# Recurrence gates of a two-layer kernel: twelve compact rows per batch, spread by transfers through memory, and one convolution product moved

## The chip, the cores and the metric

The kernel runs on one core of a Trainium2 chip. The metric is the device time of one execution in microseconds (us); the time before is the median of three executions. The engines are named as in the profile: PE is TensorE, PEld its weight load, DVE VectorE, ACT ScalarE, POOL GpSimd, and SP the engine that here issues most DMA transfers. Float32 is used throughout, and the products that need its accuracy are made as three products of a high and a low part.

## The reference, cut to what matters

Two layers, each a normalisation, an attention-like part, a second normalisation and a feed-forward part, on x of 8 batches x 512 tokens x 256. The change touches only the first part of the first layer, a rotated linear recurrence over 6 heads of 32 pairs:

```python
q, k, v = (causal_depthwise_conv(h @ W, conv) for W, conv in ...)   # [B, T, 6, 64]
theta, psi = q[..., ::2] * inv_freq, k[..., ::2] * inv_freq
alpha = sigmoid(h @ Wa)      # [B, T, 6]: one number per head and token
beta  = sigmoid(h @ Wb)      # [B, T, 6]
def step(state, inp):        # scan over the 512 tokens
    retained  = rotate(state, phi_t) * alpha_t[..., None]
    new_state = retained + beta_t[..., None] * rotate(v_t, psi_t)
    return new_state, rotate(new_state, -theta_t)
o = out * rsqrt(mean(out**2) + eps) * rms_w * silu(h @ Wg)
x = x + o @ Wo
```

alpha and beta have one value per head, but the recurrence runs on 32 pairs of each head, so the kernel needs each of them on 32 partitions. After this part come a router with 16 experts and two shared experts, then the experts' own pass, then a causal attention with 16 heads and a feed-forward part over 688 columns. None of that is changed.

## The kernel before, in words

**Units.** The first layer goes through 4 units (`NU`) of 2 batches each. A unit's 2 x 192 pair rows (6 heads x 32 pairs) are laid on 3 tiles of 128 partitions (`RT = 3`): tile 0 holds heads 0 to 3 of the first batch, tile 2 those of the second, and tile 1 (`SPLIT_ROW`) the last two heads of both, half and half. The free dimension is the 512 tokens.

**Work of a unit y, interleaved with unit x = y - 1.** PE makes for each tile r four convolution products (`conv_products`, q, k and the two halves of v, banks 0 to 3) and the gate products (`gate_products`, banks 4 and 5 in turn, in the order of the list `GATES`). A product of one tile is 6 matmuls of 512 columns; on tile 1 a convolution product is 12. `GATES` has 12 places: places 0 to 5 make the output gates (quantities 4 and 5), places 6 to 11 make alpha and beta (quantities 6 and 7), already repeated for the 32 pairs, because POOL copies each of the 12 weight columns 32 times into `w8raw` at the start. ACT reads each gate bank (`gates`): silu for the output gates; for alpha and beta tanh of half the value and then x0.5 + 0.5, into `al` and `be`. POOL multiplies cos and sin with beta (`beta_taken`), DVE rotates the values with them (`rotate`, six operations on tiles in SBUF) and runs the recurrence as two scans with `al` as the factor (`scan`). ACT squares the result (`squares`), PE sums the squares over each head (`square_sums`, 16 matmuls with 4 columns each), DVE makes the reciprocal root (`rms`), ACT spreads it (`spread_rms`, tile `rexp`), PE transposes it (`rms_turn`), DVE multiplies the gates (`gated`), PE makes the output product (`out_product`) and DVE adds it to x (`residual`). Then come the second norm, the router and the shared experts (`router_turn` to `shared_add`).

**Order.** Each engine's list of work is written out by hand; semaphores tie the engines. On PE the order around the change is: convolution of tile 0, gate places 0 to 3, `square_sums(x, 0)`, places 4 to 7, `square_sums(x, 1)`, places 8 to 11, 12 filler transposes (`clock_turns(MIDDLE_TURNS[0], 7)`, transposes of the identity whose result nobody reads), `square_sums(x, 2)`, the first two convolution products of tile 1, `rms_turn` for three tiles, the other two convolution products, output product, and so on. `al`, `be`, `cs`, `sn`, `ve` and `vo` exist once; unit y writes them when unit x has been scanned (`s_scan`). The start of the kernel is unit 0 alone, with the loads and the clearing of a 10 MB scratch tensor (`tokens_by_expert<-zero`) beside it.

Of the kernel before, what the change touches and what calls it, by code (L numbers as in the profile page):

```python
# [25 lines left out]
P = 128  # L26
# [46 lines left out]
MIDDLE_TURNS = (12, 48, 6)  # L73
# [30 lines left out]
def two_layer_program(nc, x_in, w0, wab, cw, invf, rmsw, wo0, cent, gbias, wexp, iota16, tri, tileno, wpair, fidx, lut, out):  # L104
    ctx = ExitStack()
    with ctx:  # L106
# [8 lines left out]
        x1 = nc.dram_tensor("x1_between_stages", [NB, T, D], F32, kind="Internal").ap()  # L115
        bank = [ctx.enter_context(nc.psum_tensor(f"bank{i}", [P, 512], F32)) for i in range(8)]
# [16 lines left out]
        with ExitStack() as first_layer:  # L133
            def sa(name, shape, dt=F32):
                return first_layer.enter_context(nc.sbuf_tensor(name, shape, dt))

            with ExitStack() as raw:
                w8raw = raw.enter_context(nc.sbuf_tensor("w8raw", [P, KD, 8, ROW], F32))
            ge_even, go_even = (sa(name, [P, RT, T]) for name in ("ge0", "go0"))
            w8 = [sa(f"w8_{part}", [P, KD, 8, ROW], F32R) for part in ("high", "low")]  # L140
# [19 lines left out]
            wabs = sa("wabs", [P, KD, 2, HEADS0])  # L160
# [114 lines left out]
        s_ab = sem("l0_alpha_beta")  # L275
        s_bm = sem("l0_beta_taken")
# [122 lines left out]
        GATES = ((4, 0), (5, 0), (4, 1), (5, 1), (4, 2), (5, 2), (6, 0), (7, 0), (6, 1), (7, 1), (6, 2), (7, 2))  # L399
# [35 lines left out]
        def _(sp):  # L435
# [7 lines left out]
            for dst, src in ((w8raw[:, :, 0:6, :], w0), (wabs[:], wab), (cws[:], cw), (invfs[:], invf)):  # L443
                sp.dma_start(dst, src).then_inc(s_const, 16)
# [17 lines left out]

            for u in range(NU):
                for ab in range(2):
                    sp.wait_ge(s_acc, 2 * u + ab + 1)
                    sp.dma_start(x1[2 * u + ab, :, :].rearrange("(n p) d -> p n d", p=P), xu[u % 3][ab][:]
                                 ).then_inc(s_x1s[u % 3], 16)
                if u + 3 < NU:
                    load_unit(u + 3)
                if u == NU - 2:  # L470
                    sp.wait_ge(s_pv, 12 * NU)
                    sp.wait_ge(s_pg, 12 * NU)
# [62 lines left out]
        def _(pool):  # L535
# [17 lines left out]
            for k in range(KD):  # L553
                for j in range(2):
                    pool.tensor_copy(w8raw[:, k, 6 + j, :].rearrange("p (h c) -> p h c", c=PAIRS),
                                     wabs[:, k, j, :].unsqueeze(2).to_broadcast([P, HEADS0, PAIRS]))
# [3 lines left out]
            def gate_taken(u, r):  # L560
                n = RT * u + r
                pool.wait_ge(s_scan, n + 1)
                pool.wait_ge(s_gr, 12 * u + 2 * r + 2)
# [135 lines left out]
        def _(sc):  # L699
# [54 lines left out]
            def gate_tile(u, quant):  # L754
                return (ge[u % 2], go[u % 2], al, be)[quant - 4]

# [3 lines left out]
            def gates(u, places):  # L760
                for p in places:
                    quant, r = GATES[p]
                    src = bank[4 + p % 2]
                    sc.wait_ge(s_pg, 12 * u + p + 1)
                    if quant >= 6 and u >= 1:
                        sc.wait_ge(s_scan, RT * (u - 1) + r + 1)
                    if r == SPLIT_ROW:
                        first, ab = quant - quant % 2, quant % 2
                        moves = [(gate_tile(u, first + n)[half_of(ab), r, :], src[half_of(n), :]) for n in range(2)]
                    else:  # L770
                        moves = [(gate_tile(u, quant)[:, r, :], src[:])]
                    for dst, part in moves:
                        if quant < 6:
                            ins = sc.activation(dst, part, ACT.Silu)
                        else:
                            ins = sc.activation(dst, part, ACT.Tanh, scale=0.5)
                    ins.then_inc(s_gr, 1)
                for p in places:
                    quant, r = GATES[p]
                    if quant >= 6:  # L780
                        dst = (al, be)[quant - 6][:, r, :]
                        sc.wait_ge(s_gr, 12 * u + p + 1 + (r == SPLIT_ROW and quant % 2 == 0))
                        sc.activation(dst, dst, ACT.Copy, scale=0.5, bias=0.5).then_inc(s_ab, 1)
# [39 lines left out]
            def router_input(u, turns_of=range(4)):  # L823
                for j in turns_of:
# [7 lines left out]
            def shared_silu(u, n):  # L832
# [3 lines left out]
                if n >= 2:  # L836
# [8 lines left out]
            high(w8[0][:, :, 4:8, :].rearrange("p k q n -> p k (q n)"),  # L845
                 w8raw[:, :, 4:8, :].rearrange("p k q n -> p k (q n)"), s_w8h)
# [257 lines left out]
        def _(v):  # L1104
# [319 lines left out]
            for n in range(2):  # L1424
                quants = slice(4 * n, 4 * n + 4)
                v.wait_ge(s_w8h, n + 1)
# [325 lines left out]
        def _(pe):  # L1752
# [44 lines left out]

            def conv_products(u, r, quants):
# [5 lines left out]
            def gate_products(u, places):  # L1804
                for p in places:
                    quant, r = GATES[p]
                    if p >= 2:
                        pe.wait_ge(s_gr, 12 * u + p - 1)
                    elif u == 1:
                        pe.wait_ge(s_gr, 12)  # L1810
                    elif u >= 2:
                        pe.wait_ge(s_acc, 2 * (u - 2) + 1)
                    if r == SPLIT_ROW:
# [16 lines left out]
            def rms_turn(u, r):  # L1830
                pe.wait_ge(s_re, u + 1 + (u == NU - 1 and r >= LAST_PARTS[0][1]))
                if r == 2 and u + 1 < NU:
                    pe.wait_ge(s_gr, 12 * (u + 1) + 11)
# [6 lines left out]
            def out_product(u, ab):  # L1840
                pe.wait_ge(s_y, RT * u + RT)
                if ab == 1 and u + 1 < NU:
                    pe.wait_ge(s_gr, 12 * (u + 1) + 12)
# [33 lines left out]
            def router_turn(u):  # L1877
                pe.wait_ge(s_res, 2 * u + 2)
                unit_turn(u, xm, s_xm, (6, 7, 4, 5), s_t2, (0,))
                clock_turns(MIDDLE_TURNS[2], 5)  # L1880
# [71 lines left out]
            gate_products(0, (6, 7, 8, 9, 10, 11))  # L1952
            first_turn(1)
            pe.wait_ge(s_const2, 16 * CONST2_DMAS)
            for y in range(1, NU):
# [21 lines left out]
                clock_turns(MIDDLE_TURNS[1], 6)  # L1977
# [357 lines left out]
```

## Time and profile before

| | us |
|---|---|
| median of three executions | 2203.79 |
| their lowest and highest | 2198.75, 2204.74 |
| span of the profiled execution, first to last instruction | 2190.4 |
| median less span | 13.4 |
| start and unit 0 alone | 0 to 70 |
| unit pairs y = 1, 2, 3 | 70 to 173.4, to 277.7, to 380.2 |
| last unit's rest, then the experts' pass | 380.2 to about 700 |
| second layer | about 700 to 2190 |

The profiled execution's own time is not recorded apart from its span; the 13.4 us between its span and the median are taken as what lies around a span. PE is busy 97% of the span, DVE 77%, ACT 58% and POOL 26%. The pages give start, duration, engine, line, operation, tiles and, in brackets, the idle time before an instruction with what ended it.

### The profile page before, as it was taken

How to read it: one execution, taken by the hardware profiler on the slowest of the kernel's cores; microseconds unless marked ns; L12 is line 12 of the kernel's file. 1: busy time of each engine (PE TensorE's matmuls, PEld its weight loads, DVE VectorE, ACT ScalarE, POOL GpSimd, SP SyncE). 2: the span in 40 equal slices, each digit the busy share in tenths (PEclk: the TensorE clock that was granted, in tenths of full speed). 3: DMA queues.
4: the chain of work that ended last, by engine and by line, in shares of the span. 5: the costliest groups of instructions: out<-in, count | busy, mean ns of one | idle time of the engine just before them, and what ended most of it. 6: DMA issues, size and time to landing. Idle time of an engine off the chain costs nothing. (4 is left out here: it accounts for less than half of the span.)

```text
span 2190.4 us, 37661 instructions
## 1 busy us (share of the span) xinstructions
PE 2123.2 (97%) x13038; PEld 1854.3 (85%) x13038; DVE 1694.3 (77%) x4387; ACT 1273.8 (58%) x3487; POOL 559.2 (26%) x604
## 2 busy tenths in 40 slices
PE   6899999979999999999999999999999999999997
PEld 5677777758788999899989989998998999899887
DVE  7998886887767887777876877787687778767775
ACT  5644443226637676666665666666566666656662
POOL 0214333430015323122222312222232222222220
PEclk9999999999999999999999999999999999999999
DMA  9001010436522112112111211211121121111100
GB/s 300 1 1 58 20 46 26 170 121 205 172 68 64 59 51 76 39 52 70 54 40 55 82 39 54 69 54 39 57 80 39 54 68 54 39 58 50 39 20 20
DMA packets 88556, 145.81 MB, mean 67 GB/s; under 512 B 8369, under 2 KB 55857, under 8 KB 88369
## 3 DMA queue, kind: packets, MB, share of 16 engines
q1 hardware_dynamic: 67904, 112.73, 16.1%
q0 software_dynamic: 6144, 16.79, 2.2%
q10 hardware_dynamic: 14320, 13.90, 1.9%
q8 instruction: 106, 1.74, 0.3%
q14 instruction: 82, 0.66, 0.1%
HBM read 105.63 MB, written 37.75 MB: 65 GB/s over the span
## 5 line engine op out<-in xcount | busy, mean ns | idle before, releaser
L1018 ACT ACTIVATE pr<-bank,negmax 128x128 f32<-128x128 f32 (+3 forms) x512 | 263.5, 527 | 196.6 <-DVE negmax L1599 196.6
L653 POOL TENSOR_TENSOR wo_low<-wraw_o,wo_high 128x256 fp32r<-128x256 f32 x128 | 94.5, 738 | 1105.0 <-ACT wo_high L705 1105.0
L1136 DVE TENSOR_TENSOR p_low<-bank,p_high 128x512 fp32r<-128x512 f32 (+2 forms) x384 | 190.2, 551 | 100.6 <-ACT p_high L705 100.0
L705 ACT ACTIVATE p_high<-bank 128x512 fp32r<-128x512 f32 (+2 forms) x384 | 177.4, 497 | 149.9 <-PE bank L2121 149.9
L1599 DVE CUSTOM_DVE_ANT_0 bank<-bank,causal 128x128 f32<-128x128 f32 (+3 forms) x512 | 234.7, 520 | 1.1 <-PE bank L1762 1.1
L1626 DVE SCALAR_TENSOR_TENSOR xs<-bank,rinv,xs 128x256 f32<-128x256 f32 x512 | 211.7, 474 | 1.2 <-PE bank L1762 1.2
L1760 PE MATMUL bank<-h_high,wqk_high 128*128 128x512 f32 x512 | 202.6, 396 | 0.0
L1761 PE MATMUL bank<-h_low,wqk_high 128*128 128x512 f32 x512 | 202.5, 396 | 0.0
L1762 PE MATMUL bank<-h_high,wqk_low 128*128 128x512 f32 x512 | 202.3, 395 | 0.0
L1136 DVE TENSOR_TENSOR z_low<-bank,z_high 128x512 fp32r<-128x512 f32 x128 | 88.4, 691 | 130.8 <-ACT z_high L705 130.3
L643 POOL TENSOR_TENSOR wqk_low<-wraw,wqk_high 128x512 fp32r<-128x512 f32 x128 | 165.6, 1294 | 77.3 <-ACT wqk_high L705 77.3
L2121 PEld LDWEIGHTS bank<-ident,pr 128*128 128x128 f32 x1280 | 147.6, 140 | 18.4 <-ACT pr L1018 1.3
L2121 PE MATMUL bank<-ident,pr 128*128 128x128 f32 x1280 | 160.4, 272 | 1.1 <-ACT pr L1018 1.1
L705 ACT ACTIVATE z_high<-bank 128x512 fp32r<-128x512 f32 x128 | 76.6, 599 | 138.1 <-PE bank L2132 138.1
L1760 PE MATMUL bank<-wv_high,h_high 128*128 128x256 f32 x512 | 154.8, 302 | 0.0
L1760 PE MATMUL bank<-wo_high,z_high 128*128 128x256 f32 x512 | 148.0, 289 | 2.4 <-issue 2.3
L1762 PE MATMUL bank<-wv_high,h_low 128*128 128x256 f32 x512 | 144.5, 282 | 0.0
L1762 PE MATMUL bank<-wo_high,z_low 128*128 128x256 f32 x512 | 144.1, 282 | 0.0
L1761 PE MATMUL bank<-wv_low,h_high 128*128 128x256 f32 x512 | 144.0, 281 | 0.0
L1761 PE MATMUL bank<-wo_low,z_high 128*128 128x256 f32 x512 | 143.8, 281 | 0.0
L1760 PE MATMUL bank<-k_high,q_high 128*128 128x384 f32 (+2 forms) x384 | 140.8, 367 | 0.0
L1760 PE MATMUL bank<-p_high,v_high 128*128 128x512 f32 (+2 forms) x384 | 131.2, 342 | 2.4 <-DVE p_low L1136 2.3
(338 smaller groups left out, 6327.3 us busy)
## 6 DMA issues: line engine op xcount, KB each, us to landing
wraw<-in_wpair SPq DMA_DIRECT2D x64, 512.0 KB, 4.0
wraw<-in_wpair SPq DMA_DIRECT2D x64, 256.0 KB, 4.4
wraw_o<-in_wpair SPq DMA_DIRECT2D x64, 256.0 KB, 2.5
tokens_by_expert<-zero SPq DMA_DIRECT2D x10, 1024.0 KB, 11.2
xt<-tokens_by_expert SPq DMA_DIRECT2D x40, 256.0 KB, 3.3
expert_results<-ey ACTq DMA_DIRECT2D x40, 256.0 KB, 3.7
wres<-in_wexp SPq DMA_DIRECT2D x1, 6144.0 KB, 20.7
xs<-x_between_stages SPq DMA_DIRECT2D x8, 512.0 KB, 4.5
```

The source lines that it names most:

```text
L643: pool.tensor_tensor(low, wraw[r][:, 2 * e * D:2 * (e + 1) * D], high.bitcast(F32), ALU.subtract).then_inc(s_wq, 1)
L653: pool.tensor_tensor(wo2[e][1][:], wraw_o[r][:, e, :], wo2[e][0][:].bitcast(F32), ALU.subtract).then_inc(s_wo, 1)
L705: sc.activation(dst, src, ACT.Copy, scale=scale).then_inc(done, 1)
L1018: ins = sc.activation(pr[:, i, 0:(i + 1) * P], score(i), ACT.Exp, scale=-1.0, bias=negmax[:, i:i + 1], accum_out=rsum[:, i:i + 1])
L1136: v.tensor_tensor(at(parts[1]), src, high_, ALU.subtract).then_inc(done, 1)
L1599: ins = v.tensor_tensor_reduce(score(i), score(i), causal[:, (NT - 1 - i) * P:NT * P], -1.0, -NEG, ALU.add, ALU.min, negmax[:, i:i + 1])
L1626: ins = v.scalar_tensor_tensor(xb[:, i, :], bank[6 + n][:, (i % 2) * D:(i % 2 + 1) * D], rinv[:, i:i + 1], xb[:, i, :], ALU.mult, ALU.add)
L1760: mm(dst, w[0], x[0], start=start, stop=False)
L1761: mm(dst, w[0], x[1], start=False, stop=False)
L1762: return mm(dst, w[1], x[0], start=False, stop=stop)
L2121: ins = pe.transpose(bank[2 + n][:, at:at + P], pr[:, i, j * P:(j + 1) * P], ident[:])
```

## The change

alpha and beta are no longer made on all pair rows. Their 12 weight columns (6 for alpha, 6 for beta) are kept as they are, padded to 64 columns (`wab2`), and one product of 6 matmuls per batch gives 12 rows of 512 tokens. ACT applies the same tanh and x0.5 + 0.5 to these 12 rows (`alpha_beta`, into `ab_rows`, which lies in the first 12 partitions of `hm`). SP stores the rows of a unit in a small tensor in memory (`ab_heads`), waits until they are there, waits until `al` and `be` are free, and loads them back with eight transfers (`spread_alpha_beta`), each of which reads every row 32 times, so that they fill `al` and `be`. `beta_taken` waits for all eight. `GATES` has 8 places. POOL's four copies of weight columns are gone, the conversions of the weights are smaller, and the 12 filler transposes are gone. On PE the products of q and k of tile 1 (`conv_products(y, 1, (0, 1))`) are issued ahead of `square_sums(x, 2)` instead of behind it, and ACT reads them behind `squares(x, 2)`, where it did before. A tensor `room` keeps the addresses behind the smaller weights where they were.

```diff
-MIDDLE_TURNS = (12, 48, 6)
+MIDDLE_TURNS = (48, 6)
+        ab_heads = nc.dram_tensor("alpha_beta_by_head", [2, 2, HEADS0, T], F32, kind="Internal").ap()
...
-                w8raw = raw.enter_context(nc.sbuf_tensor("w8raw", [P, KD, 8, ROW], F32))
+                w8raw = raw.enter_context(nc.sbuf_tensor("w8raw", [P, KD, 6, ROW], F32))
+                wabs = raw.enter_context(nc.sbuf_tensor("wabs", [P, KD, P // 2], F32))
+            wab2 = [sa(f"wab_{part}", [P, KD, P // 2], F32R) for part in ("high", "low")]
+            sa("room", [P, 10 * P])
+            ab_rows = hm[0:2 * HEADS0, 0]
...
-        GATES = ((4, 0), (5, 0), (4, 1), (5, 1), (4, 2), (5, 2), (6, 0), (7, 0), (6, 1), (7, 1), (6, 2), (7, 2))
+        GATES = ((4, 0), (5, 0), (4, 1), (5, 1), (4, 2), (5, 2), (6, 0), (6, 1))
+        NG0 = len(GATES)
+        AB_PIECES = ((0, 0, P, 0, 0, 4), (1, 0, P // 2, 0, 4, HEADS0), (1, P // 2, P, 1, 4, HEADS0), (2, 0, P, 1, 0, 4))
+        AB_DMAS = 2 * len(AB_PIECES)
...
+            def spread_alpha_beta(u):
+                sp.wait_ge(s_ab, 2 * u + 2)
+                sp.wait_ge(s_abr, 16 * AB_DMAS * u)
+                sp.dma_start(ab_heads.rearrange("b q h t -> (q h) b t"), ab_rows).then_inc(s_abw, 16)
+                sp.wait_ge(s_abw, 16 * (u + 1))
+                if u >= 1:
+                    sp.wait_ge(s_scan, RT * u)
+                    sp.wait_ge(s_bm, RT * u)
+                for q, dst in enumerate((al, be)):
+                    for r, p0, p1, ab, h0, h1 in AB_PIECES:
+                        sp.dma_start(dst[p0:p1, r, :],
+                                     ab_heads[ab, q, h0:h1, :].unsqueeze(1).to_broadcast([h1 - h0, PAIRS, T])
+                                     ).then_inc(s_abr, 16)
+
+            spread_alpha_beta(0)
             for u in range(NU):
+                if u + 1 < NU:
+                    spread_alpha_beta(u + 1)
...
             def beta_taken(u, r):
                 pool.wait_ge(s_trig, RT * u + r + 1)
-                pool.wait_ge(s_ab, 6 * u + 2 * r + 2)
+                pool.wait_ge(s_abr, 16 * AB_DMAS * (u + 1))
...
+            def alpha_beta(u):
+                if u >= 1:
+                    sc.wait_ge(s_abw, 16 * u)
+                    sc.wait_ge(s_su, 4 * max(u - 1, 0))
+                for ab in range(2):
+                    p = 6 + ab
+                    sc.wait_ge(s_pg, NG0 * u + p + 1)
+                    sc.activation(ab_rows[:, ab, :], bank[4 + p % 2][0:2 * HEADS0, :], ACT.Tanh, scale=0.5).then_inc(s_gr, 1)
+                for ab in range(2):
+                    sc.wait_ge(s_gr, NG0 * u + 7 + ab)
+                    sc.activation(ab_rows[:, ab, :], ab_rows[:, ab, :], ACT.Copy, scale=0.5, bias=0.5).then_inc(s_ab, 1)
...
             def router_input(u, turns_of=range(4)):
+                sc.wait_ge(s_abw, 16 * min(u + 2, NU))
...
-            gates(0, (6, 7))
+            alpha_beta(0)
             whole_turns(0, 2)
-            gates(0, (8, 9))
             input_high(1)
             sin_cos(0, 2)
-            gates(0, (10, 11))
...
                 squares(x, 1)
-                gates(y, (6, 7))
-                gates(y, (8, 9))
-                gates(y, (10,))
+                alpha_beta(y)
                 squares(x, 2)
-                gates(y, (11,))
                 tap_angle(y, 1)
                 spread_rms(x)
...
+            def alpha_beta_product(dst, ab):
+                for k in range(KD):
+                    ins = mm3(dst[0:P // 2, :], parts(wab2, lambda t: t[:, k, :]), parts(hT2, lambda t: t[:, ab, k, :]),
+                              k == 0, k == KD - 1)
+                return ins
...
-            gate_products(0, (6, 7, 8, 9, 10, 11))
+            gate_products(0, (6, 7))
             first_turn(1)
...
                 gate_products(y, (4, 5, 6, 7))
                 square_sums(x, 1)
-                gate_products(y, (8, 9, 10, 11))
-                clock_turns(MIDDLE_TURNS[0], 7)
+                conv_products(y, 1, (0, 1))
                 square_sums(x, 2)
-                conv_products(y, 1, (0, 1))
                 for r in range(RT):
                     rms_turn(x, r)
```

## Rows read from the trace of the kernel before

**Rows 1.** Stretches: busy time of each engine, granted PE clock, DMA share, GB/s.

```profile
core 0: us, PE busy (x) PEld busy (x) DVE busy (x) ACT busy (x) POOL busy (x), PEclk, DMA share, GB/s
0.00:70.00 70.00, 48.31 (x205) 37.10 (x206) 57.45 (x122) 42.73 (x73) 9.68 (x22) 1.00 0.71 234
70.00:173.40 103.40, 97.49 (x498) 75.05 (x498) 91.00 (x190) 50.12 (x87) 25.06 (x41) 0.98 0.01 3
```

**Rows 2.** DVE timeline, pairs y = 1, 2, 3: around rms and residual.

```profile
105.38 0.21 DVE L1125 SCALAR_TENSOR_TENSOR ry<-rt,ry 128x48 f32<-128x48 f32 x1
107.95 2.32 DVE L1180 SCALAR_TENSOR_TENSOR ang<-bank,cws,ang 128x511 f32<-128x511 f32 x3 [2.37 <-ACT ang L723]
...
134.07 1.29 DVE L1274 TENSOR_TENSOR xs<-bank,xs 128x512 f32<-128x512 f32 x2 [1.90 <-PE bank L1855]
...
208.27 0.21 DVE L1125 SCALAR_TENSOR_TENSOR ry<-rt,ry 128x48 f32<-128x48 f32 x1
...
311.47 0.21 DVE L1258 TENSOR_SCALAR va<-bank 128x48 f32<-128x48 f32 x1 [1.39 <-PE bank L1827]
```

**Rows 3.** PE and ACT timelines: the roots' transposes of the three pairs, and the spread.

```profile
109.80 1.47 PE L1836 MATMUL bank<-ident,rexp 128*128 128x128 f32 x12
...
211.28 1.47 PE L1836 MATMUL bank<-ident,rexp 128*128 128x128 f32 x12
...
316.89 1.47 PE L1836 MATMUL bank<-ident,rexp 128*128 128x128 f32 x12
...
107.81 1.48 ACT L797 ACTIVATE rexp<-ry 128x1536 f32<-128x1536 f32 x1
```

**Rows 4.** Stretches as in rows 1: same products warm and cold, two more falls.

```profile
102.80:109.80 7.00, 7.00 (x26) 4.85 (x27) 4.04 (x14) 2.57 (x4) 0.00 (x0) 0.79 0.00 0
205.70:211.30 5.60, 5.60 (x27) 3.91 (x27) 4.20 (x15) 2.57 (x4) 4.09 (x5) 1.00 0.23 94
...
249.40:256.00 6.60, 6.60 (x14) 3.70 (x15) 4.59 (x22) 3.69 (x5) 2.48 (x2) 0.50 0.00 0
```

**Rows 5.** PE timeline, pair 1: last sums of squares, whose start waited for ACT.

```profile
100.78 0.38 PE L1826 MATMUL bank<-headsum,sq 128*128 128x4 f32 x2 [0.78 <-ACT sq L791]
```

**Rows 6.** ACT and POOL timelines, unit 0: last step of beta, then POOL's use.

```profile
57.98 0.64 ACT L783 ACTIVATE be<-be 128x512 f32<-128x512 f32 x1
...
58.77 1.29 POOL L572 TENSOR_TENSOR cs<-cs,be 128x512 f32<-128x512 f32 x1 [46.57 <-ACT be L783]
60.02 1.26 POOL L572 TENSOR_TENSOR sn<-sn,be 128x512 f32<-128x512 f32 x1
...
71.48 1.40 POOL L572 TENSOR_TENSOR cs<-cs,be 128x512 f32<-128x512 f32 x1 [4.23 <-ACT be L783]
72.85 1.73 POOL L572 TENSOR_TENSOR sn<-sn,be 128x512 f32<-128x512 f32 x1
```

**Rows 7.** DVE timeline, 69 to 88 us: first rotation beside POOL, second without.

```profile
69.85 0.67 DVE L1228 TENSOR_TENSOR tt<-ve,cs 128x512 f32<-128x512 f32 x1
...
71.65 1.78 DVE L1231 TENSOR_TENSOR tt<-ve,sn 128x512 f32<-128x512 f32 x1
73.47 1.66 DVE L1232 TENSOR_TENSOR tt<-tt 128x512 f32<-128x512 f32 x1
75.05 0.68 DVE L1233 TENSOR_TENSOR tt<-tt 128x512 f32<-128x512 f32 x1
...
83.48 0.69 DVE L1228 TENSOR_TENSOR tt<-ve,cs 128x512 f32<-128x512 f32 x1
...
87.34 1.22 DVE L1240 TENSOR_TENSOR_SCAN oe<-al,tt 128x512 f32<-128x512 f32 x1
```

**Rows 8.** DMA issues to 440 us (KB each, median us to landing); one issue on SP.

```profile
x_between_stages<-xs SPq DMA_DIRECT2D x3, 512.0 KB, 3.0
...
tokens_by_expert<-xm,slots POOLq DMA_INDIRECT x48, 2.4
...
8.84 0.43 SPq L449 DMA_DIRECT2D luts<-in_lut  x1
```

**Rows 9.** Stretches as in rows 1: rate of plain transfers, and of indirect ones.

```profile
30.00:50.00 20.00, 20.00 (x88) 14.88 (x87) 18.85 (x45) 12.98 (x25) 0.00 (x0) 1.00 1.04 341
...
207.00:208.00 1.00, 1.00 (x6) 0.60 (x5) 0.85 (x5) 0.00 (x0) 0.74 (x1) 1.00 0.32 131
```

More of the change, by code:

```diff
@@ L137, in two_layer_program @@
             with ExitStack() as raw:
-                w8raw = raw.enter_context(nc.sbuf_tensor("w8raw", [P, KD, 8, ROW], F32))
+                w8raw = raw.enter_context(nc.sbuf_tensor("w8raw", [P, KD, 6, ROW], F32))
+                wabs = raw.enter_context(nc.sbuf_tensor("wabs", [P, KD, P // 2], F32))
             ge_even, go_even = (sa(name, [P, RT, T]) for name in ("ge0", "go0"))
-            w8 = [sa(f"w8_{part}", [P, KD, 8, ROW], F32R) for part in ("high", "low")]
+            w8 = [sa(f"w8_{part}", [P, KD, 6, ROW], F32R) for part in ("high", "low")]
+            wab2 = [sa(f"wab_{part}", [P, KD, P // 2], F32R) for part in ("high", "low")]
+            sa("room", [P, 10 * P])
             ge_odd, go_odd = (sa(name, [P, RT, T]) for name in ("ge1", "go1"))
@@ L159, in two_layer_program @@
             wo_rest = sa("wo_rest", [P, 2, D])
-            wabs = sa("wabs", [P, KD, 2, HEADS0])
             cws = sa("cws", [P, 2, 4, TAPS])
@@ L275, in two_layer_program @@
         s_ab = sem("l0_alpha_beta")
+        s_abw = sem("l0_alpha_beta_stored")
+        s_abr = sem("l0_alpha_beta_spread")
         s_bm = sem("l0_beta_taken")
@@ L442, in _ @@
             load_unit(0)
-            for dst, src in ((w8raw[:, :, 0:6, :], w0), (wabs[:], wab), (cws[:], cw), (invfs[:], invf)):
+            for dst, src in ((w8raw[:], w0), (wabs[:], wab), (cws[:], cw), (invfs[:], invf)):
                 sp.dma_start(dst, src).then_inc(s_const, 16)
@@ L471, in _ @@
                     sp.wait_ge(s_pv, 12 * NU)
-                    sp.wait_ge(s_pg, 12 * NU)
+                    sp.wait_ge(s_pg, NG0 * NU)
                     for c in range(EARLY_CHUNKS):
@@ L552, in _ @@
             pool.wait_ge(s_const, 16 * CONST_DMAS)
[L553 to L556, printed above, removed]
             pool.tensor_scalar(cws[:, :, 0], cws[:, :, 0], invfs[:, 0:1], -1.0, ALU.mult, ALU.mult)
@@ L562, in gate_taken @@
                 pool.wait_ge(s_scan, n + 1)
-                pool.wait_ge(s_gr, 12 * u + 2 * r + 2)
+                pool.wait_ge(s_gr, NG0 * u + 2 * r + 2)
                 for gate, scanned in ((ge, oe), (go, oo)):
@@ L752, in sin_cos @@
                 sc.activation(cs[:, r, :], turns[n % 2][:], ACT.Sin, scale=-1.0, bias=half_pi[:]).then_inc(s_trig, 1)
-            def gate_tile(u, quant):
-                return (ge[u % 2], go[u % 2], al, be)[quant - 4]
             def half_of(n):
@@ L763, in gates @@
                     src = bank[4 + p % 2]
-                    sc.wait_ge(s_pg, 12 * u + p + 1)
-                    if quant >= 6 and u >= 1:
-                        sc.wait_ge(s_scan, RT * (u - 1) + r + 1)
+                    sc.wait_ge(s_pg, NG0 * u + p + 1)
                     if r == SPLIT_ROW:
-                        first, ab = quant - quant % 2, quant % 2
-                        moves = [(gate_tile(u, first + n)[half_of(ab), r, :], src[half_of(n), :]) for n in range(2)]
+                        ab = quant % 2
+                        moves = [(gate[u % 2][half_of(ab), r, :], src[half_of(n), :]) for n, gate in enumerate((ge, go))]
                     else:
-                        moves = [(gate_tile(u, quant)[:, r, :], src[:])]
+                        moves = [((ge, go)[quant - 4][u % 2][:, r, :], src[:])]
                     for dst, part in moves:
[L773 to L776, printed above, removed]
+                        ins = sc.activation(dst, part, ACT.Silu)
                     ins.then_inc(s_gr, 1)
[L778 to L783, printed above, removed]
+            def alpha_beta(u):
[4 more added lines that the diff above has]
+                    p = 6 + ab
+                    sc.wait_ge(s_pg, NG0 * u + p + 1)
+                    sc.activation(ab_rows[:, ab, :], bank[4 + p % 2][0:2 * HEADS0, :], ACT.Tanh, scale=0.5).then_inc(s_gr, 1)
+                for ab in range(2):
+                    sc.wait_ge(s_gr, NG0 * u + 7 + ab)
+                    sc.activation(ab_rows[:, ab, :], ab_rows[:, ab, :], ACT.Copy, scale=0.5, bias=0.5).then_inc(s_ab, 1)
             def squares(u, r):
@@ L844, in _ @@
             sc.wait_ge(s_setup, 2)
-            high(w8[0][:, :, 4:8, :].rearrange("p k q n -> p k (q n)"),
-                 w8raw[:, :, 4:8, :].rearrange("p k q n -> p k (q n)"), s_w8h)
+            high(wab2[0][:], wabs[:], s_w8h)
+            high(w8[0][:, :, 4:6, :].rearrange("p k q n -> p k (q n)"),
+                 w8raw[:, :, 4:6, :].rearrange("p k q n -> p k (q n)"), s_w8h)
             input_high(0)
@@ L1424, in _ @@
             for n in range(2):
-                quants = slice(4 * n, 4 * n + 4)
-                v.wait_ge(s_w8h, n + 1)
+                quants = slice(4 * n, min(4 * n + 4, 6))
+                v.wait_ge(s_w8h, 2 * n + 1)
+                if n == 1:
+                    v.tensor_tensor(wab2[1][:], wabs[:], wab2[0][:].bitcast(F32), ALU.subtract)
                 v.tensor_tensor(w8[1][:, :, quants, :], w8raw[:, :, quants, :], w8[0][:, :, quants, :].bitcast(F32),
@@ L1807, in gate_products @@
                     if p >= 2:
-                        pe.wait_ge(s_gr, 12 * u + p - 1)
+                        pe.wait_ge(s_gr, NG0 * u + p - 1)
                     elif u == 1:
-                        pe.wait_ge(s_gr, 12)
+                        pe.wait_ge(s_gr, NG0)
                     elif u >= 2:
                         pe.wait_ge(s_acc, 2 * (u - 2) + 1)
-                    if r == SPLIT_ROW:
+                    if quant == 6:
+                        alpha_beta_product(bank[4 + p % 2], r).then_inc(s_pg, 1)
+                    elif r == SPLIT_ROW:
                         rests_product(bank[4 + p % 2], quant - quant % 2, quant % 2).then_inc(s_pg, 1)
@@ L1832, in rms_turn @@
                 if r == 2 and u + 1 < NU:
-                    pe.wait_ge(s_gr, 12 * (u + 1) + 11)
+                    pe.wait_ge(s_gr, NG0 * (u + 1) + NG0 - 1)
                 for i in range(NT):
@@ L1842, in out_product @@
                 if ab == 1 and u + 1 < NU:
-                    pe.wait_ge(s_gr, 12 * (u + 1) + 12)
+                    pe.wait_ge(s_gr, NG0 * (u + 1) + NG0)
                 half = slice(ab * P // 2, (ab + 1) * P // 2)
@@ L1879, in router_turn @@
                 unit_turn(u, xm, s_xm, (6, 7, 4, 5), s_t2, (0,))
-                clock_turns(MIDDLE_TURNS[2], 5)
+                clock_turns(MIDDLE_TURNS[1], 5)
                 unit_turn(u, xm, s_xm, (6, 7, 4, 5), s_t2, (1,))
@@ L1976, in _ @@
                 pe.wait_ge(s_res, 2 * x + 1)
-                clock_turns(MIDDLE_TURNS[1], 6)
+                clock_turns(MIDDLE_TURNS[0], 6)
                 router_turn(x)
@@ L2279 @@
     w0 = kt(w0.reshape(D, -1)).reshape(P, KD, 6, ROW)
-    wab = kt(np.concatenate([a["L0_attn_Wa"], np.roll(a["L0_attn_Wb"], HEADS0 - P // PAIRS, -1)], 1)).reshape(P, KD, 2, HEADS0)
+    wab = kt(np.concatenate([a["L0_attn_Wa"], a["L0_attn_Wb"], np.zeros((D, P // 2 - 2 * HEADS0), np.float32)], 1))
     cq, ck, cv = (a["L0_attn_conv_" + c].T for c in "qkv")
```

## The prediction, made blind

> **What bounds the kernel now.** I read the page's busy shares first, then the stretches, then the timelines of DVE, PE, ACT and POOL side by side. Only the first layer, the first 480 us or so, can change. In the start and in the pairs y = 1 to 3 the engine that sets the pace is mostly DVE: 91.00 of 103.4 us busy in pair 1 [rows 1], and without a gap from 70 to 102.7 us. Then there is a place where the pace passes to PE. In pair 1 the chain of the reciprocal root ends at 105.59 (105.38 + 0.21), DVE waits 2.37 us for the q angle of tile 1, and later 1.90 us for the output product before the second residual [rows 2]. Between, PE runs without a gap from the roots' transposes at 109.80 [rows 3] to that product. So what counts in a pair is how early PE can start `rms_turn`; everything behind moves with it, because PE's 48 filler transposes that come later only fill a wait for DVE's second norm. ACT and POOL have slack, so the ten ACT instructions per unit that disappear are worth nothing by themselves: what hides them is DVE's unbroken work.
>
> **PE's work.** Places 8 to 11 go: 4 x 6 = 24 matmuls, and 12 filler transposes. The 24 matmuls of the moved products q and k take their place; a run of 24 takes 5.6 us warm with what is around it [rows 4]. The alpha-beta products at places 6 and 7 stay at 6 matmuls each, as long as before, since the columns streamed are still 512. Up to `square_sums(x, 2)` PE has thus the same work, less the fillers, and all of this lies under DVE's rotations. The gain is behind the sums: PE no longer has 5.6 us (7.0 in pair 1) between sums and transposes.
>
> **The pairs' gain.** `rms_turn` now waits for the root and its spread alone: the end of DVE's chain, 0.1 us to ACT, 1.48 us for `rexp` [rows 3], 0.1 us to PE, so 1.7 us behind the chain's end.
> Pair 1: DVE's wait of 0.30 us before the chain goes too (the sums start earlier, ACT being free for the squares at once, where PE waited 0.78 us [rows 5]). Chain end 105.59 - 0.3 = 105.3; transposes at 107.0 instead of 109.80 [rows 3]: 2.8 us.
> Pair 2: chain end 208.48 [rows 2]; transposes at 210.2 instead of 211.28: 1.1 us.
> Pair 3: the chain starts without its wait of 1.39 us [rows 2]. In the same distances it ends at 312.7, transposes at 314.4 instead of 316.89: 2.5 us.
> Sum 6.4 us, if PE's clock holds. DVE is not in the way: it does the q angle (2.3 us) and the gates while PE does its products, and the 1.90 us of waiting at the residual say that PE has to be earlier first.
>
> **The clock.** The same moved products take 7.0 us at a mean granted clock of 0.79 in pair 1 and 5.6 us at 1.00 in pair 2 [rows 4]: a fall to the lower level (1.2 GHz) costs 1.4 us there. It fell behind a wait of 0.78 us followed by the 4-column matmuls [rows 5], and behind the same pattern in pair 2 it did not. Now PE has, behind those sums, nothing at all from about 101.5 to 107.0, five to six us without fillers. I take it that the clock is down at `rms_turn` in each pair. The price of one fall lies between 1.4 us (dense products) and 3.3 us, half of the 6.6 us that it stayed at 0.50 at 249.4 [rows 4]; I take 1.8 us, nearer the first, because dense products follow. Three falls: 5.4 us. Falls elsewhere I keep as they are. The pairs thus give 6.4 - 5.4 = 1.0 us. Bounds: 6.4 us gained, 3.5 us lost.
>
> **The start, where cover is missing.** In unit 0 there is no earlier unit under which the way through memory could hide. beta of tile 0 was ready at 58.62 (57.98 + 0.64) and used by POOL at 58.77 [rows 6]; the rotation began at 69.85 [rows 7]. Now ACT has the 12 rows of both batches at about the same 58.6: the same two products before it and the same four instructions, whose length goes by the 512 columns and not by the partitions. Then, on SP, whose queue is idle there (the clearing has been issued by 46 us and landed by 53):
> - the store, 48 KB: between 2.4 and 3.0 us to landing [rows 8]; I take 3.0, at 61.7 with SP's wake-up.
> - eight loads, 0.43 us each to issue [rows 8], the last at 65.1; 1.57 MB at 341 GB/s need 4.6 us, at 131 GB/s 12.0 us [rows 9]. With some 2.5 us from first issue to first data and landing, 68.3 by the first; by the second 61.7 + 12.0 + about 1 = 74.7. No row has a load that reads a row 32 times. I take the first rate, since these are plain transfers with 2 KB pieces issued by SP, and the slow one is POOL's indirect scatter, which its issue paces.
> - POOL's two multiplications, 2.5 us [rows 6]: cos and sin ready at 70.9. The rotation starts at 70.9 instead of 69.85: 1.0 us lost. DVE itself would be ready about 68, because the last angle reduction no longer runs beside POOL.
> - what is late next: tiles 1 and 2 of beta come now straight behind, so four POOL instructions fall on the first rotation's six DVE operations instead of two. Rows: the six operations took 5.9 us (69.85 to 75.76) with two POOL instructions beside them and 3.9 us (83.48 to 87.34) with none, so 1.0 us for each [rows 7, 6]. Four cost 4.1 instead of 2.0: 2.1 us lost.
>
> The start loses 3.1 us. The smaller weight conversions (768 + 128 columns instead of 1536 on ACT and DVE) and POOL's four copies give nothing I would count: DVE's first angle waits for PE's first product.
>
> The Trainium skill (SBUF — State Buffer, section "SBUF: two separate sides") says that the pair of ports that DVE and GpSimd share is an exclusive lock, held for the whole instruction, also against DVE operations with two SBUF inputs. By that rule each POOL instruction would hold DVE for its full 1.27 us, four for 5.1 us, and the sum would be 0.9 us higher. The rows show alternation as the rule has it, and 1.0 us for each, which I use. The same skill (DMA: Bandwidth & Descriptors, section "Anatomy of one DMA — SWDGE (gpsimd) path") puts the fixed cost of a transfer at about 2.0 us, most of it completion. By that figure the small store would land 1.0 us earlier, and the sum would be as much lower.
>
> **Later units' transfers.** SP sends the store of unit y at about 93 us in pair 1, waits for the third scan at 98.3 and the eight loads land by 105; `beta_taken` needs the first cosine at about 109. Even at the slow rate (111) only POOL waits, and the rotation comes 65 us later. Behind SP's new waits stand the x1 stores and the load of unit 3, which wait anyway for `shared_add` at 171 us. So 0. The wait in `router_input` for the store is long past. Without this cover the price would be that of the start.
>
> **Sum.** +3.1 - 1.0 = +2.1 us on the span of 2190.4, so 2192.5; with the 13.4 us around it 2205.9, against the median of 2203.8.
>
> **The rivals.**
> *A. The spread is slow (slower).* Loads that read one row 32 times go at 131 GB/s or below: landing at 74.7, 6.4 us later than above, all on DVE's path: +8.5, 2212.3. It decides from a landing at 72.8 on. For it: no row shows such a load. Against it: 341 GB/s for plain transfers, idle queues. Chance 0.18.
> *B. The clock holds at `rms_turn`.* In pair 2 it held over a short gap. Then 6.4 gained, 3.1 lost: -3.3, 2200.5; if the loads also land by the time DVE is ready, the start loses 1 us and it is -5.4. Against it: the gap is now many times as long. Chance 0.15.
> *C. The falls at the router move.* The clock fell at 249.4 and not at the same place of pair 1, so everything that shifts by some us may add or remove one; DVE lost about 2.8 us by it. Two fewer: -5.6 + 2.1 = -3.5, 2200.3; with B in any pair beyond that. One or two more: +4.9 to +7.7, 2208.7 to 2211.5. Chance 0.10 for fewer, 0.07 for more.
> *D. The likeliest*, the sum above, 2200 to 2212 by its own bounds: 0.50.
>
> **Chances and range.** 0.3%, 6.6 us, is about what a measurement here can tell from no change: the three runs lie 6 us apart. Faster by more needs parts of B and C together: 0.12. Slower by more: most of A, some of C's second half and the dear end of D, 0.25. Between: 0.63. The range that holds 8 in 10 reaches from B and C together with one fall fewer (2200.5 - 2.8, 2197.7) to A with falls at 2.4 us instead of 1.8 (2212.3 + 1.8, 2214.1): 2197 to 2214.
>
> **What the changed profile would show.** The store of `ab_heads` issued near 58.7, the last load landed near 68, POOL's six multiplications of unit 0 in one row from there, and the first rotation from about 71 to 79 with several operations near 1.7 us. In each pair: no wait before the q angle, `rms_turn` 1.7 us behind the root's chain, about 5 us of idle PE ahead of it, and a granted clock of 0.5 for some us behind it; the second residual still waiting for PE. Behind 480 us nothing. The prediction is wrong if the loads land after 72.8, if the clock stays at 1.00 at the transposes, or if the number of falls at the router differs.

## The result, and the profile after

The changed kernel takes 2226.7 us (2225.8 to 2230.6, 4 runs) against 2201.9 us for the kernel before in the same series (4 runs): ratio 1.0112, 95% interval [1.0099, 1.0125], which on a time of 2198 us is 24.6 us slower. The forecast was 2205.9, and its range ended at 2214. Every execution after takes 1.7 us more than its span (2225.81 and 2224.1 in the profiled one). So the trace of before, span 2190.4, was of an execution near 2192, 4 to 10 us under the medians that this kernel shows in the four series (2195.8 to 2201.9); the 13.4 us of the forecast were mostly that. Differences between traces thus overstate a loss by some 6 us. Below, losses of whole kernels go by the ratios; stretches inside a kernel are read from single traces.

The trace shows two places. The first is unit 0. SP's timeline of after has store and loads (the last column but one is how many transfers a row holds):

```profile
57.62 0.37 SPq L475 DMA_DIRECT2D alpha_beta_by_head<-hm  x1
59.46 2.47 SPq L482 DMA_DIRECT2D al<-alpha_beta_by_head  x4
61.98 9.45 SPq L482 DMA_DIRECT2D be<-alpha_beta_by_head  x4
```

Stretches of after, while the loads run (the last three numbers are the granted PE clock, the DMA share and GB/s):

```profile
63.00:68.00 5.00, 5.00 (x20) 4.59 (x21) 4.35 (x7) 3.11 (x6) 0.00 (x0) 0.52 0.26 99
76.00:78.00 2.00, 0.00 (x0) 0.00 (x0) 0.00 (x0) 0.00 (x0) 0.00 (x0) 1.00 0.13 51
80.00:82.00 2.00, 0.00 (x0) 0.00 (x0) 0.00 (x0) 0.00 (x0) 0.00 (x0) 0.50 0.12 46
```

A share of 0.26 is 4 of the 16 DMA engines, 0.13 is 2. The pieces of 4 heads (1.05 MB) and of 2 heads (0.52 MB) take 1.05/0.100 + 0.52/0.051, about 10.5 + 10.3 = 20.8 us, from 61 to 82. This sums the pieces as if they ran one after another. The stretches don't follow the order of the pieces (0.26 up to 69 us, 0.13 to 72, about 0.26 to 75, 0.13 to 82), so some overlap. If the same two engines take part in every piece, each carries 8 x 65.5 KB, and at 25 GB/s that is 21.0 us, as long. Which engine carried what isn't shown. POOL's timeline of after has the first use of beta, DVE's the first rotation, the answer to [rows 6, 7]:

```profile
82.56 1.26 POOL L594 TENSOR_TENSOR cs<-cs,be 128x512 f32<-128x512 f32 x1 [72.17 <-DMA be<-alpha_beta_by_head]
```

```profile
85.08 1.73 DVE L1245 TENSOR_TENSOR tt<-ve,cs 128x512 f32<-128x512 f32 x1 [17.07 <-POOL sn L594]
86.74 1.74 DVE L1246 TENSOR_TENSOR tt<-vo,sn 128x512 f32<-128x512 f32 x1
...
91.85 0.69 DVE L1249 TENSOR_TENSOR tt<-tt 128x512 f32<-128x512 f32 x1
```

DVE is ready at 68.0 and waits 17.07 us; before, it had rotated since 69.85. Four of six operations then take 1.74 us beside POOL.

The second place is pairs 2 and 3. POOL's timeline of after in pair 2, then ACT's, PE's and DVE's:

```profile
245.78 1.28 POOL L594 TENSOR_TENSOR cs<-cs,be 128x512 f32<-128x512 f32 x1 [15.38 <-DMA be<-alpha_beta_by_head]
247.03 1.26 POOL L594 TENSOR_TENSOR sn<-sn,be 128x512 f32<-128x512 f32 x1
248.46 1.01 POOL L605 DMA_INDIRECT tokens_by_expert<-xm,slots  x1 [0.16 <-issue]
...
262.40 0.96 POOL L605 DMA_INDIRECT tokens_by_expert<-xm,slots  x1 [0.31 <-issue]
```

```profile
264.80 2.08 ACT L734 ACTIVATE xm<-xs,nbu,ryu 128x256 f32<-128x256 f32 x4 [6.93 <-DMA tokens_by_expert<-xm,slots]
```

```profile
267.02 1.94 PE L1798 MATMUL bank<-ident,xm 128*128 128x128 f32 x8 [4.64 <-ACT xm L734]
```

```profile
275.92 0.29 DVE L1309 TENSOR_SCALAR bia<-bank 128x128 f32<-128x128 f32 x1 [6.39 <-PE bank L1914]
```

Read downwards this is one chain. Ten of the 16 scatters of unit y-2 stand behind the late beta in POOL's program; they read `xm`, so `router_norm` of unit y-1 can't write it; PE waits for the transposes' input, DVE for the logits. Pair 1 has no scatters and is hardly longer.

In each pair the roots' transposes, the answer to [rows 3], take 2.8 us instead of 1.47, with the granted clock at 0.50 (PE's timeline of after; stretches of after behind the first):

```profile
125.05 2.83 PE L1863 MATMUL bank<-ident,rexp 128*128 128x128 f32 x12 [4.28 <-ACT rexp L817]
...
228.48 2.82 PE L1863 MATMUL bank<-ident,rexp 128*128 128x128 f32 x12 [5.26 <-ACT rexp L817]
...
338.17 2.82 PE L1863 MATMUL bank<-ident,rexp 128*128 128x128 f32 x12 [5.13 <-ACT rexp L817]
```

```profile
123.00:129.00 6.00, 3.95 (x16) 3.66 (x17) 5.37 (x10) 3.14 (x4) 0.00 (x0) 0.50 0.22 79
129.00:133.00 4.00, 4.00 (x18) 2.81 (x17) 3.86 (x7) 0.69 (x1) 0.00 (x0) 0.97 0.21 80
```

### The profile page after: what moved, and what is told of

Read it like the earlier page. It is cut to its first block and busy times, and to the rows that moved or that the text cites. A ratio compares the mean times of both kernels' runs of the same rounds, so it can differ in the third digit from the quotient of the medians.

```text
span 2224.1 us, 37388 instructions
## 1 busy us (share of the span) xinstructions
PE 2115.3 (95%) x12906; PEld 1845.9 (83%) x12906; DVE 1695.3 (76%) x4388; ACT 1249.6 (56%) x3448; POOL 558.5 (25%) x600
## 6 DMA issues: line engine op xcount, KB each, us to landing
wres<-in_wexp SPq DMA_DIRECT2D x1, 6144.0 KB, 20.8
```

## The experiments

All are compared with the kernel before on the same chip. "First scan" is the start of the odd scan of tile 0 in unit 0 on DVE's timeline, the pairs are the distances to the same scan of units 1, 2 and 3, and the last stretch is from there to the first `xt` transposes on PE. These are of one trace each. "Loss" is (ratio - 1) x 2198 us, so a width of 0.0018 in an interval is 4 us.

| kernel | first scan | pairs 1, 2, 3 | last stretch | ratio [95%] | loss |
|---|---|---|---|---|---|
| before | 76.9 | 103.1, 104.3, 102.5 | 90.4 | | |
| the change | 94.3 | 104.0, 109.9, 105.8 | 94.9 | 1.0112 [1.0099, 1.0125] | 24.6 |
| e1 wide stores | 84.9 | 103.3, 103.0, 102.8 | 90.4 | 1.0012 [1.0002, 1.0021] | 2.6 |
| e2 move alone | 77.0 | 109.0, 107.3, 102.8 | 93.9 | 1.0053 [1.0036, 1.0069] | 11.6 |
| e3 e1 + fillers | 84.5 | 102.9, 100.4, 98.5 | 92.3 | 1.0011 [1.0001, 1.0021] | 2.4 |
| e4 scatters first | 94.5 | 103.6, 102.9, 102.7 | 90.4 | 1.0060 [1.0039, 1.0081] | 13.2 |
| e5 e1 without the move | 84.6 | 106.5, 103.5, 102.5 | 92.0 | 1.0033 [1.0019, 1.0047] | 7.3 |
| e6 a load per head | 84.1 | 103.7, 102.9, 102.7 | 90.4 | 1.0006 [0.9995, 1.0018] | 1.3 |
| e7 early alpha-beta | 74.7 | 105.6, 105.8, 102.7 | 90.3 | 0.9981 [0.9970, 0.9992] | -4.2 |
| e8 e7 + fillers | 74.6 | 101.6, 100.3, 98.5 | 92.4 | 0.9961 [0.9946, 0.9977] | -8.6 |
| e9 two copies | 86.4 | 102.7, 102.8, 100.3 | 92.1 | one run, 2201.7 against 2198.1 | |
| e10 slow loads in unit 0 alone | 94.3 | 103.1, 102.9, 99.5 | 90.5 | 1.0046 [1.0028, 1.0064] | 10.1 |
| e11 slow loads in units 1 to 3 alone | 83.5 | 103.1, 109.7, 106.3 | 90.4 | 1.0059 [1.0041, 1.0077] | 13.0 |

**e1, wide stores.** Two stores write each of the 12 rows 8 times; the loads' outer dimension becomes 32 or 16.

```
+for ab in range(2):
+    sp.dma_start(ab_heads[ab]..., ab_rows[:, ab, :].unsqueeze(1).to_broadcast([2 * HEADS0, 8, T]))
-ab_heads[ab, q, h0:h1, :].unsqueeze(1).to_broadcast([h1 - h0, PAIRS, T])
+ab_heads[ab, q, h0:h1, :, :].rearrange("h c t -> (h c) t").unsqueeze(1).to_broadcast([(h1 - h0) * 8, PAIRS // 8, T])
```

> The changed kernel, but the store writes each of the 12 rows eight times into memory and each load reads rows 16 or 32 deep in its outer dimension (repeated 4 times instead of 32). Same bytes loaded, 1.57 MB per unit, eight loads as before. Theory 1 (a load runs on as many DMA engines as its outer dimension, 4 heads or 2, allows; the profile shows 0.26 and 0.13 of the engines busy at 100 and 50 GB/s): the busy share goes above 0.8, the last load of unit 0 lands between 66 and 71 us instead of 82.5, the first rotation starts near 70 to 72 instead of 85, the scatters of units 2 and 3 are no longer late, and the time is 2200 to 2207. Theory 2 (reading the same memory row again and again is what is slow): the rate stays near 100 GB/s at best, the landing stays behind 78 us and the time behind 2218.

Stretches of e1, stores and then loads, and PE's timeline:

```profile
59.00:64.00 5.00, 1.08 (x5) 1.11 (x6) 4.79 (x7) 0.28 (x1) 0.00 (x0) 0.50 0.67 77
...
66.00:72.00 6.00, 6.00 (x25) 4.85 (x24) 1.61 (x3) 3.18 (x6) 0.00 (x0) 0.85 0.77 259
```

```profile
114.82 2.82 PE L1865 MATMUL bank<-ident,rexp 128*128 128x128 f32 x12 [5.30 <-ACT rexp L819]
```

The share rises from 0.26 and 0.13 to 0.77 in the mean while the loads run, beta is taken at 73.04 instead of 82.56, and 22.0 of the 24.6 us are gone. The share of above 0.8 and the landing by 71 were missed, though not by much. The wider stores take until 64 us, so the loads are issued from 64.64 on instead of 59.46.

**e2, the move alone**, in the kernel before: `conv_products(y, 1, (0, 1))` ahead of `square_sums(x, 2)`, without the 12 fillers.

> The kernel before with one part of the change alone: the products of q and k of tile 1 ahead of the last sums of squares, and the 12 filler transposes gone; alpha and beta as before. If the step of the prediction holds, the roots' transposes start 1.1 to 2.8 us earlier in each pair and a fall of the clock behind the idle stretch takes about 1.8 us of it back each time: 2198 to 2203 against some 2202 for the kernel before. If the clock's fall costs more than the earlier start gives (up to 3.3 us each), 2203 to 2207. If the clock holds: 2195 to 2197.

DVE's waits in e2 (us in total, times, the longest):

```profile
DVE va L1258 <- PE bank L1827: 13.9, 3, 6.2
```

All three expected times were too low (2207.5 beside 2195.8). With the 24 matmuls of places 8 to 11 still there, the moved ones make the sums late and DVE waits for them, which the expectation had left out. The move needs the compact rows.

**e3, fillers.** e1 with `clock_turns(38, 7)` between `square_sums(x, 2)` and `rms_turn`.

> As the kernel with wide loads, and 38 filler transposes (4.3 us) between the last sums of squares and the roots' transposes of each pair, where PE is idle. If the clock's fall at that place costs what I think, the granted clock is 1.00 at the roots' transposes and the time 4 to 6 us below that of the kernel with wide loads. If the fall costs nothing (DVE sets the pace there), equal within 2 us.

In these two traces the pairs shrink by 7.2 us in all, 2.4 for each fall avoided. The time hardly moves: by the medians e3 is 0.7 us faster than e1 (2197.28 and 2197.93), where 4 to 6 were expected. The last stretch takes 1.9 us more, and what comes after the layer 2 us more (2195.8 - 478.6 = 1717.2 against 2199.4 - 484.3 = 1715.1). The trace of e1 is also of an execution 3.2 us above its median, so the 2.4 us may be too high.

**e4, the scatters first.** The change, but POOL issues all 16 scatters ahead of the multiplications by beta.

> The changed kernel with narrow loads, but in the pairs 2 and 3 POOL issues all 16 scatters of the earlier unit ahead of the three multiplications with beta instead of between them. Theory A (the late beta holds POOL, behind it stand the scatters, and ACT may not overwrite xm before they are done): ACT's wait for the scatters (6.9 us in pair 2) goes, and the time falls by 5 to 10 us to 2217 to 2222; the start stays as late as it is. Theory B (the late scatters cost nothing, the loss behind the start is the clock's): within 2 us of 2226.7.

PE's waits in e4, and the change's wait for the same input beside it:

```profile
PE bank L1798 <- ACT xm L734: 0.5, 3, 0.2
```

```profile
PE bank L1798 <- ACT xm L734: 8.0, 4, 4.6
```

The chain through POOL's queue is shown: betas come as late as in the change, the first scan too, and pairs 2 and 3 are 103 us long. It is worth 11.4 us (24.6 - 13.2), more than the 5 to 10 expected.

**e5, no move.** e1 with the moved products back behind the sums, without fillers.

> Compact rows with every row stored eight times (so that the loads' outer dimension is 16 or 32), and the products q and k of tile 1 back behind the last squares' sums; the 12 fillers stay out. Theory (the cost of the compact rows is the wait of unit 0 for beta, and the move by itself is worth about 1 us): start as in the run with wide stores, first scan about 8 us later than before, and the pairs about as long as before's (sum 309 to 311 us), rms_turn with a clock of 1.00 because products lie ahead of it; the whole 0 to 3 us slower than the wide run with the move. Rival (the move costs more than it gives, by the clock at rms_turn): the pairs shorter than the wide run's by 3 us or more, and the whole faster than it by as much.

e5 is 4.7 us slower than e1, more than the 0 to 3 expected: with compact rows the move gives some 5 us, though it lets the clock fall. In e5 the roots' transposes take 0.27 us each, in e1 0.42.

**e6, a load per head.** The change's single store, then 24 loads.

```
-sp.dma_start(dst[p0:p1, r, :], ab_heads[ab, q, h0:h1, :].unsqueeze(1).to_broadcast([h1 - h0, PAIRS, T]))
+for h in range(h0, h1):
+    p = p0 + PAIRS * (h - h0)
+    sp.dma_start(dst[p:p + PAIRS, r, :], ab_heads[ab, q, h:h + 1, :].to_broadcast([PAIRS, T]))
```

> The change with its single store of 48 KB, but 24 loads of one head each (outer dimension 32, 64 KB) instead of eight loads of 2 or 4 heads. Theory (a transfer's rate goes by how its outer dimension divides over the 16 engines: 4 heads 100 GB/s, 2 heads 50 GB/s in the change): issue sets the pace, 24 x 0.43 = 10.3 us from about 60, so the last lands near 73, the later units' beta comes in time, and the kernel is within 4 us of the wide run and some 25 us faster than the change. Rival (a load that reads a row 32 times is slow as such, whatever its shape): 1.57 MB at 50 to 100 GB/s again, landing at 80 or later, and a time near the change's.

Stretch of e6 while its loads run:

```profile
62.00:72.00 10.00, 8.90 (x38) 7.86 (x39) 5.39 (x9) 4.62 (x8) 0.00 (x0) 0.73 0.53 138
```

The same bytes, the same rows read 32 times, from the same 48 KB, now at 138 GB/s: 64 KB every 0.46 us, the pace of issue. Reading a row 32 times isn't what was slow. POOL takes beta at 72.28. Nearly the whole loss is gone.

**e9, two copies.** e1 with 2 copies of each row, so that the outer dimension is 8 or 4.

> As the run with wide stores, but every row stored twice, so that the loads' outer dimension is 8 for the pieces of 4 heads and 4 for those of 2. Theory (the outer dimension sets how many of the 16 DMA engines carry a load): 4-head pieces at a DMA share near 0.5 and 200 GB/s, 2-head pieces at 0.25 and 100 GB/s, twice the change's rates; 1.05 MB and 0.52 MB take 5.2 + 5.2 = 10.4 us instead of 20.8, beta of tile 0 is taken by POOL near 73, first scan 84 to 86. Rival (reading a row many times from memory is slow by the repeated reads, not by the shape): the shares stay at 0.26 and 0.13, the landing near 80.

```profile
66.00:70.00 4.00, 4.00 (x16) 3.18 (x15) 1.72 (x3) 3.39 (x6) 0.00 (x0) 0.70 0.51 178
...
72.00:74.00 2.00, 2.00 (x10) 1.65 (x9) 0.00 (x0) 0.00 (x0) 0.00 (x0) 1.00 0.25 90
```

Twice the change's shares. Outer dimension 2, 4, 8 gives shares of 0.13, 0.26, 0.51. The theory expected these, with the landing a little earlier (POOL takes beta at 74.66).

**e10 and e11, the two halves.** The change's eight loads in unit 0 alone, or in units 1 to 3 alone; elsewhere a load per head.

> The change with its eight loads in unit 0 and 24 loads of one head each in the units 1 to 3. Theory (the change loses in two places: some 15 us at the start, and 10 to 13 us where late betas hold POOL and with it the scatters of the unit before): the first scan late as in the change, 94 to 95, the pairs 103 to 104 us each, 2208 to 2213, as the run with the scatters first. Rival (the scatters' order mattered, not the late betas): pairs as long as the change's and a time near 2225.

> The other half: 24 loads of one head each in unit 0, the change's eight loads in the units 1 to 3. Theory: first scan at 84, pairs 2 and 3 longer than 103 us by what the change showed there (109.9 and 105.8), last stretch 94 to 95, 2208 to 2213: the two losses add up to the change's. Rival (the late betas only hurt because unit 0 had already been late): pairs near 103 and a time near that of 24 loads everywhere, 2198.

POOL's waits from 90 us on, e10 and then e11:

```profile
POOL cs L606 <- DMA be<-alpha_beta_by_head: 17.8, 3, 11.6
```

```profile
POOL cs L606 <- DMA be<-alpha_beta_by_head: 51.3, 3, 20.6
```

Against e6 the slow loads cost 8.8 us in unit 0 and 11.7 us in the later units; with e6's own 1.3 this makes 21.8 of the 24.6 us. The intervals of e10 and e11 reach 4 us to either side, so the remaining 2.8 us are not clear of noise. e11 shows that late betas in later units hurt by themselves, without a late start. Its last stretch was expected at 94 to 95 us, as in the change, and took 90.4.

**e7, alpha-beta early.** e1 with the alpha-beta products as places 0 and 1 of a unit, and unit 0's store and loads issued ahead of the clearing.

```
-GATES = ((4, 0), (5, 0), (4, 1), (5, 1), (4, 2), (5, 2), (6, 0), (6, 1))
+GATES = ((6, 0), (6, 1), (4, 0), (5, 0), (4, 1), (5, 1), (4, 2), (5, 2))
+spread_alpha_beta(0)
 for n in range(NTILE // 8):
     sp.dma_start(xsort[...], zero[...])
```

> Wide stores, and the alpha-beta product as the first instead of the last of the eight gate products of a unit, with unit 0's store and loads issued ahead of the clearing of the sorted tokens. Theory (what the compact rows cost at the start is that nothing lies over their way through memory): beta lands before DVE is ready to rotate; the first rotation starts at 70 or earlier and the first scan is back near before's 76.9; pairs as in the wide run (309.0 in all); some 7 us faster than the wide run, so 2188 to 2193, 3 to 7 us faster than the kernel before. Rival: the clearing, now some 10 us later, or the gates of the second and third tile, now later, hold DVE or POOL instead, and nothing is won over the wide run.

POOL's timeline of e7:

```profile
44.78 1.28 POOL L596 TENSOR_TENSOR cs<-cs,be 128x512 f32<-128x512 f32 x1 [34.35 <-DMA be<-alpha_beta_by_head]
```

The way through memory is hidden, and the first scan starts 2.2 us earlier than before. Against e1 it wins 10.2 us there and 6.8 by the ratios; its pairs are 5 us longer than e1's, where they were expected to be equal, and no run tells why.

**e8, the same with fillers**: `clock_turns(38, 7)` as in e3.

> As the run before, with 38 filler transposes between the last squares' sums and rms_turn. Theory (the fall of the clock at rms_turn costs 1.8 us in each pair or more): the pairs take 302 to 305 us instead of 309, and 2182 to 2190 in all. Rival (what is won in the pairs is given back where the last unit waits for something else, as in the wide run with fillers): the pairs shorter, the end of the layer not, and a time equal to the run without fillers.

Stretches around `rms_turn` in the three pairs, e7 and then e8:

```profile
100.00:115.00 15.00, 10.43 (x40) 8.19 (x41) 13.68 (x28) 4.44 (x7) 2.52 (x2) 0.66 0.20 65
205.00:220.00 15.00, 9.67 (x37) 7.50 (x38) 13.59 (x28) 3.82 (x5) 12.15 (x12) 0.66 0.43 150
310.00:325.00 15.00, 9.65 (x40) 7.58 (x40) 13.77 (x29) 3.83 (x5) 12.21 (x13) 0.66 0.47 169
```

```profile
100.00:115.00 15.00, 15.00 (x84) 12.94 (x82) 13.91 (x29) 5.67 (x8) 2.55 (x2) 0.89 0.18 60
205.00:220.00 15.00, 14.18 (x72) 11.17 (x71) 14.51 (x21) 5.41 (x8) 10.01 (x10) 1.00 0.24 94
310.00:325.00 15.00, 15.00 (x67) 11.77 (x66) 14.34 (x24) 4.91 (x8) 8.10 (x8) 1.00 0.11 44
```

The mean clock is 0.66 without fillers and 0.89 to 1.00 with them. The pairs shrink by 13.6 us in these two traces, but the medians differ by 5.4 (2191.96 and 2186.55); the trace of e7 is of an execution 4.1 us above its median. e7 and e8 both beat the kernel before. e8 is the faster, 2186.6 us, and even the upper end of its interval is 0.23% under the kernel before. Why the same fillers gave 5.4 us here and 0.7 in e3 isn't shown.

## Why the prediction was wrong, step by step

The forecast said +2.1 us, the ratio says +24.6. The error of 22.5 us has three parts that the runs measure: 14.3 at the start, 11.7 in the later units, and 4.2 the other way in the pairs. That makes 21.8; the rest is within the noise.

**The rate of the loads: the step that failed.** "I take the first rate, since these are plain transfers with 2 KB pieces issued by SP": 341 GB/s, landing at 68.3. Measured: 100 and 51 GB/s, POOL released at 82.56. The row it rested on [rows 9] is of the clearing, stores from 128 partitions; these are loads with an outer dimension of 4 or 2. Rival A had the direction and a landing "from 72.8 on" as its point of decision, but the wrong mechanism and a rate that was still too good. e6 and e9 show the mechanism: same bytes and rows, other outer dimension, other share. The Trainium skill (DMA: Bandwidth & Descriptors, section "Why a DMA increments its semaphore by 16 and not by 1") states it: a transfer runs on the largest number of engines up to 16 that divides the slowest dimension of both sides. By that rule 4 heads give 4 engines and 2 heads 2, and the traces agree (0.26 and 0.13 of 16). With the 25 GB/s for each engine that the trace shows (100/4), this accounts for the 20.8 us. The prediction cited the page and missed this rule.

**The rest of the start was right.** Four POOL multiplications beside the rotation were to cost 4.1 us where two had cost 2.0; in e6, where the rotation runs from 74.84 to the scan at 82.95, it takes 8.1 us against 3.9 alone [rows 7], so 4.2. That bears out the 1.0 us for each that the prediction took from its rows, and not the 5.1 us, the whole length of four POOL instructions, that it set beside them by the Trainium skill (SBUF — State Buffer, section "SBUF: two separate sides"). The store was faster than forecast: the loads are issued 1.8 us behind it, not 3.0. The 2.0 us that it cited beside its 3.0 from the Trainium skill (DMA: Bandwidth & Descriptors, section "Anatomy of one DMA — SWDGE (gpsimd) path") came nearer, though that section is on transfers that GpSimd issues, and this store went through SP's queue. The whole start was to lose 3.1 and lost 17.4 (94.3 against 76.9).

**"Later units' transfers: 0" failed too.** "Even at the slow rate (111) only POOL waits" counted pair 1 alone, at a rate that was too high, and did not name what is queued behind the waiting instruction in pairs 2 and 3: the scatters, which hold `xm`. e4 takes the queue's order away and e11 the late start; 11.7 us.

**The pairs: right mechanisms, sizes off.** No wait before the q angle, transposes 1.6 us behind the chain (e1: 113.20 to 114.82; forecast 1.7), five idle us ahead of them and the clock at 0.50 in all three pairs: all as written. Rival B did not occur. In single traces a fall costs 2.4 us by e3 against e1 instead of 1.8, and the gain without falls is 8.0 us (309.8 - 301.8) instead of 6.4. In the traces the net is -0.8, beside a forecast of -1.0. That was luck: gain and falls were both too small, and the two errors cancel (8.0 - 7.2 against 6.4 - 5.4). By the ratios it is larger: e1, e4 and e6 start 8.0, 17.6 and 7.2 us late and lose 2.6, 13.2 and 1.3, so everything behind the first scan gives 4.4 to 5.9 us against a typical execution of the kernel before. The mean is 5.2, 4.2 more than forecast. Which part of before is longer in its typical execution than in its trace isn't shown.

**The sum by measured terms:** 17.4 - 5.2 + 11.7 = 23.9, of 24.6. The 17.4 is from traces; by the ratios alone the parts make 21.8 (e10 and e11).

**What stays open.** The change's last stretch is 4.5 us longer than in e4, e10 or e11. Nearly all of it is one wait of DVE at the last `shared_add`, for which the profile names none of the core's engines:

```profile
500.30 1.29 DVE L1390 SCALAR_TENSOR_TENSOR xs<-bank,xs 128x512 f32<-128x512 f32 x2 [4.23 <-remote]
```

This is one execution of the change; whether its others have this wait isn't known.

Rival C's second half, one or two more falls at the router move, occurred at least once. In pair 1 the granted clock was 1.00 at the shared experts' first products (148.6 to 154.6 us) before; at the same products it is 0.72 in the change (165.9 to 171.9 us). Its price can't be told apart. From the first scan to the experts' pass the mean granted clock is 0.97 before, 0.90 in the change, 0.92 in e1 and 0.95 in e3. Times that differ by a few us can't settle it either: single executions of one kernel differ by 0.4 us (e10) to 11 us (e8).

## What to carry to other kernels

Read a DMA's rate off a row of the same shape, its outer dimension above all: a load that spreads 4 rows over 128 partitions is the rate of 4 engines, whatever its bytes, and cutting it into one transfer per row, or storing each row several times first, gives the others back. Where an instruction gets a new wait, write down everything behind it in its engine's program in each pass of the loop, not in the first alone. A detour through memory is free only where other work lies over it: moving the product that feeds it to the front of the unit, and its first transfers ahead of the clearing, turned a loss into a gain. Fillers where PE has been emptied ahead of a join kept the clock up in both kernels that had them, but the time fell clearly in one alone (5.4 us in e8, 0.7 in e3), so measure them in each kernel.

## What the runs showed of the hardware

- Shares of 0.13, 0.26 and 0.51 for transfers whose outer dimension is 2, 4 and 8: some 22 to 25 GB/s for each engine.
- SP was held while it issued: four loads took it 9.45 us in the change and 2.53 us in e1. It seems that slow transfers ahead make the issues themselves wait; no run was made for that.
- Two stores of 12 partitions that write each row 8 times ran at 77 GB/s with a DMA share of 0.67, some 5 us before the loads could start.
- A POOL and a DVE operation of 128x512, 1.26 and 0.69 us alone, take 1.71 and 1.74 us each when they alternate over several instructions.
